# A graph network's diffusion layer: fp16 parts for the logits, keys by four tiles, and another order on TensorE, ScalarE and GpSimd

## What is computed

```python
q = X @ W1.T @ W2.T
k = X @ W3.T
logits = q @ k.T / TAU
probs = jax.nn.softmax(logits, axis=-1)
...
keep_sorted = cs - sp < TOP_P
...
for n in range(STEPS):
    A = _top_p_attention(Xa, W1, W2, W3)
    Xf = R @ Xf
    Xa = A @ Xa
    Z = Z + Xf @ U1[n].T + Xa @ U2[n].T
```

## Time and profile before

| | us |
|---|---|
| median of 3 runs | 3413.45 (3412.4 to 3425.25) |
| the profiled execution | 3413.29 |
| its span | 3411.6 |
| PE, PEld busy | 2529.9 (74%), 1807.8 (53%) |
| DVE, ACT, POOL busy | 2115.1 (62%), 1274.7 (37%), 618.0 (18%) |
| keys0, from 854.8 | 89.1 |
| step0, from 944.9 | 696.1 |
| keys1, from 1642.5 | 95.4 |
| step1, from 1738.9 | 928.1 |

### The profile page before, as it was taken

How to read it: one execution, slowest core, us unless ns; L and a number is a source line. 1 busy time by engine, 2 the same in 40 slices (tenths; PEclk the granted TensorE clock), 3 DMA queues, 4 the chain that set the end, 5 groups by cost and what they waited for, 6 DMA issues and landing times. The chain is left out here.

```text
span 3411.6 us, 47607 instructions
## 1 busy us (share of the span) xinstructions
PE 2529.9 (74%) x14938; PEld 1807.8 (53%) x14938; DVE 2115.1 (62%) x5159; ACT 1274.7 (37%) x2109; POOL 618.0 (18%) x1525
## 2 busy tenths in 40 slices
PE   3488888496848998887843596397757149999999
PEld 2366666385616776666622475275546124444458
DVE  5567777613236666675137777877776667777751
...
DMA packets 44330, 104.10 MB, mean 31 GB/s; under 512 B 5584, under 2 KB 24304, under 8 KB 41328
## 3 DMA queue, kind: packets, MB, share of 16 engines
...
## 5 line engine op out<-in xcount | busy, mean ns | idle before, releaser
L1206 PE MATMUL bank<-kT,step_queries 64*128 64x512 f32 x528 | 285.4, 693 | 315.0 <-ACT step_E L1273 299.5
L1705 DVE SCALAR_TENSOR_TENSOR fil_acc<-bank,fil_node,fil_acc 128x256 f32<-128x256 f32 x682 | 330.0, 484 | 108.6 <-PE bank L1778 96.0
L1206 PEld LDWEIGHTS bank<-kT,step_queries 64*128 64x128 f32 x528 | 107.5, 228 | 491.0 <-ACT step_E L1273 413.0
L1273 ACT ACTIVATE step_E<-bank 128x512 f32<-128x512 f32 (+1 forms) x264 | 137.5, 545 | 413.0 <-PE bank L1206 210.3
L1776 PE MATMUL bank<-fil_wh,fil_xTh 128*128 128x512 f16 x704 | 267.5, 380 | 0.0
L1777 PE MATMUL bank<-fil_wl,fil_xTh 128*128 128x512 f16 x704 | 267.3, 380 | 0.0
L1778 PE MATMUL bank<-fil_wh,fil_xTl 128*128 128x512 f16 x704 | 267.2, 380 | 0.0
L1293 ACT ACTIVATE step_junk<-step_E,step_first 128x2708 fp8e4<-128x2708 f32 x88 | 224.6, 2552 | 14.7 <-ACT step_bell L1300 8.9
L1386 DVE MAX8 step_top<-step_E 128x8 f32<-128x2708 f32 x44 | 131.2, 2982 | 133.1 <-ACT step_E L1273 128.6
L1223 PE MATMUL bank<-H,step_PT 128*128 128x256 f32 x968 | 212.6, 379 | 0.8 <-ACT step_PT L1264 0.8
L1223 PE MATMUL bank<-A,step_PT 128*128 128x256 f32 x968 | 212.6, 379 | 0.7 <-ACT step_PT L1264 0.7
...
## 6 DMA issues: line engine op xcount, KB each, us to landing
...
```

Source lines behind the costliest of these rows:

```text
L1206: pe.matmul(l_bank[n % 2][:, 0:m], queries[q][half, :], kT[half, c:c + m], start=True, stop=True).then_inc(l_ready, 1)
L1273: act.activation(E[q][j][:, c:c + m], l_bank[n % 2][:, 0:m], ACT.Copy).then_inc(l_done, 1)
L1705: c(dve.scalar_tensor_tensor(out=acc[k][:], in0=ps, scalar=node[k][:, n:n + 1], in1=acc[k][:], op0=ALU.mult, op1=ALU.add))
```

## The change

There are four parts.

1. `keys` stages four tiles at a time and, instead of kT and qT, keeps keys and queries as fp16 parts scaled by 64: kH and kL for the keys (high and low, the same 64 rows twice), and qHL, whose rows 0 to 63 are the high part of the query and rows 64 to 127 the low part. The second loop works on three tiles at a time, and the additions into H stand in the first loop.
2. `logits`: two fp16 products over 128 rows (qHL with kH, qHL with kL) for each fp32 one over 64; ACT scales by 1/4096 as it evacuates. POOL's `query` goes.
3. PE's order: two chunks of logits, a third of the neighbours, two chunks, a third, two chunks, a third, transposes, turn, half of attend, mix, the other half.
4. ACT's second sums stand ahead of the exponentials, and POOL's secant ahead of guess. The first sums are written at the head of the list with another lag.

DVE's list in `diffusion_step` is untouched. The diff, cut:

```diff
+            def product(n):
+                k, (b, m) = n % 2, CHUNKS[n]
+                w = m * 128
+                pe.wait_ge(xT_ready, n * 2 + 2)
+                pe.wait_ge(q1_done, n)
+                for c in range(2):
+                    last = pe.matmul(q1_bank[0:DA, 0:w], w1[:, c * DA:c * DA + DA], xT[k][:, c * BANK:c * BANK + w],
+                                     start=c == 0, stop=c == 1)
+                last.then_inc(q1_ready, 1)
...
+                pe.wait_ge(k_lo, n)
+                for c in range(2):
+                    last = pe.matmul(k_bank[:, 0:w], wk[:, c * 128:c * 128 + 128], xT[k][:, c * BANK:c * BANK + w],
+                                     start=c == 0, stop=c == 1)
+                last.then_inc(k_ready, 1)
+
+            def query(n):
+                k, (b, m) = n % 2, CHUNKS[n]
+                pe.wait_ge(q1_done, n + 1)
+                pe.wait_ge(q_lo, n)
+                pe.wait_ge(q_done, n)
+                pe.matmul(q_bank[:, 0:m * 128], w2[:], q1[k][:, 0:m * 128], start=True, stop=True).then_inc(q_ready, 1)
...
+            for n in range(NCH + 1):
+                if n < NCH:
+                    transposes(n)
+                if n > 0:
+                    query(n - 1)
+                    gram_sum(n - 1)
+                if n < NCH:
+                    product(n)
...
+            def high(n):
+                b, m = CHUNKS[n]
+                act.wait_ge(k_ready, n + 1)
+                act.activation(span(kH, b, m), k_bank[:, 0:m * 128], ACT.Copy, scale=SQ).then_inc(k_hi, 1)
+
+            def query_high(n):
+                b, m = CHUNKS[n]
+                act.wait_ge(q_ready, n + 1)
+                act.activation(span(qHL, b, m), q_bank[:, 0:m * 128], ACT.Copy, scale=SQ).then_inc(q_hi, 1)
...
+            def keep_query(n):
+                b, m = CHUNKS[n]
+                w = m * 128
+                dve.wait_ge(q_hi, n + 1)
+                part = qHL[DA:, b * 128:b * 128 + w]
+                dve.scalar_tensor_tensor(out=part, in0=q_bank[DA:, 0:w], scalar=SQ, in1=part,
+                                         op0=ALU.mult, op1=ALU.subtract).then_inc(q_lo, 1)
+                dve.tensor_scalar(qT[:, b * 128:b * 128 + w], q_bank[0:DA, 0:w], 1.0, None,
+                                  ALU.mult).then_inc(q_done, 1)
+
...
-            def query(p, q):
-                if not (isinstance(p, int) and p < 2):
-                    pool.wait_ge(l_ready, (p * 2 - 2) * NL)
-                pool.tensor_copy(queries[q][:], cols(qT, p, 128)).then_inc(q_ready, 1)
...
+            guess_0, guess_1 = ((0, lambda p, q, j=j: guess(p, q, j)) for j in range(2))
             if evals == 1:
-                pipelined(pool, [(-1, query), (0, lambda p, q: guess(p, q, 0)), (0, lambda p, q: newton(p, q, 0, final, aim, ready)),
-                                 (0, lambda p, q: guess(p, q, 1)), (0, lambda p, q: newton(p, q, 1, final, aim, ready))],
-                          T // 2)
+                newton_0 = (0, lambda p, q: newton(p, q, 0, final, aim, ready))
+                newton_1 = (1, lambda p, q: newton(p, q, 1, final, aim, ready))
+                pipelined(pool, [newton_1, guess_0, newton_0, guess_1], T // 2)
             else:
-                pipelined(pool, [(-1, query), (0, lambda p, q: guess(p, q, 0)), (1, lambda p, q: secant(p, q, 1, final, aim, ready)),
-                                 (0, lambda p, q: newton(p, q, 0, second, 0.0, aimed)),
-                                 (0, lambda p, q: guess(p, q, 1)), (0, lambda p, q: secant(p, q, 0, final, aim, ready)),
-                                 (0, lambda p, q: newton(p, q, 1, second, 0.0, aimed))], T // 2)
+                newton_0 = (0, lambda p, q: newton(p, q, 0, second, 0.0, aimed))
+                newton_1 = (1, lambda p, q: newton(p, q, 1, second, 0.0, aimed))
+                secant_0 = (0, lambda p, q: secant(p, q, 0, final, aim, ready))
+                secant_1 = (1, lambda p, q: secant(p, q, 1, final, aim, ready))
+                pipelined(pool, [newton_1, secant_1, guess_0, newton_0, secant_0, guess_1], T // 2)
...
-                half = slice(j * DA, j * DA + DA)
-                if n == 0 and j == 0:
-                    pe.wait_ge(q_ready, p + 1)
-                pe.matmul(l_bank[n % 2][:, 0:m], queries[q][half, :], kT[half, c:c + m],
-                          start=True, stop=True).then_inc(l_ready, 1)
-
-            def neighbours(p, j):
+                for part, k in enumerate((kH, kL)):
+                    last = pe.matmul(l_bank[n % 2][:, 0:m], cols(qHL, t, 128), k[:, c:c + m],
+                                     start=part == 0, stop=part == 1)
+                last.then_inc(l_ready, 1)
+
+            def neighbours(p, j, n):
                 t = p * 2 + j
-                moved(pe, a8_loaded, t, j)
-                reuse(pe, u_added, t)
-                core.fence(pe)
                 ps = pvf_bank[j][:, D:]
-                for part, ap in enumerate((hi, lo)):
-                    pe.matmul(ps, core.idh[:], ap(srcF, t), start=part == 0, stop=False)
-                adjacency_times(pe, ps, a8[j], srcF, start=False)
-
-            def attend(p, j):
+                if n == 0:
+                    moved(pe, a8_loaded, t, j)
+                    reuse(pe, u_added, t)
+                    core.fence(pe)
+                    for part, ap in enumerate((hi, lo)):
+                        pe.matmul(ps, core.idh[:], ap(srcF, t), start=part == 0, stop=False)
+                for i in range(T * n // 3, T * (n + 1) // 3):
+                    for part, ap in enumerate((hi, lo)):
+                        pe.matmul(ps, a8[j][:, i * 128:i * 128 + 128], ap(srcF, i), start=False,
+                                  stop=i == T - 1 and part == 1)
+
+            def attend(p, j, n):
                 t = p * 2 + j
-                pe.wait_ge(pT_done, t * NCH + NCH)
-                for i in range(T):
+                pe.wait_ge(pT_done, t * NCH + (NCH // 2 if n == 0 else NCH))
+                for i in range(T * n // 2, T * (n + 1) // 2):
                     last = pe.matmul(pvf_bank[j][:, 0:D], PT[:, i * 128:i * 128 + 128], srcA[:, i * D:i * D + D],
                                      start=i == 0, stop=i == T - 1)
-                last.then_inc(pv_ready, 1)
+                if n == 1:
+                    last.then_inc(pv_ready, 1)
...
-            def chunks(j):
-                for n in range(NL):
-                    yield 0, lambda p, q, n=n: logits(p, q, j, n)
+            def all_transposes(p, j):
                 for n in range(NCH):
-                    yield 2, lambda p, q, n=n: transposes(p, j, n)
-
-            pipelined(pe, [(2, lambda p, q: neighbours(p, 0)), *chunks(0), (3, lambda p, q: turn(p, 1)),
-                           (3, lambda p, q: mix(p, 1)), (2, lambda p, q: attend(p, 0)),
-                           (2, lambda p, q: neighbours(p, 1)), *chunks(1), (2, lambda p, q: turn(p, 0)),
-                           (2, lambda p, q: mix(p, 0)), (2, lambda p, q: attend(p, 1))], T // 2)
+                    transposes(p, j, n)
+
+            def half(j, mixed):
+                rows = [(2, lambda p, q, n=n: neighbours(p, j, n)) for n in range(3)]
+                chunks = [(0, lambda p, q, n=n: logits(p, q, j, n)) for n in range(NL)]
+                return [*chunks[0:2], rows[0], *chunks[2:4], rows[1], *chunks[4:], rows[2],
+                        (2, lambda p, q: all_transposes(p, j)), (mixed, lambda p, q: turn(p, 1 - j)),
+                        (2, lambda p, q: attend(p, j, 0)), (mixed, lambda p, q: mix(p, 1 - j)),
+                        (2, lambda p, q: attend(p, j, 1))]
+
+            pipelined(pe, [*half(0, 3), *half(1, 2)], T // 2)
...
-                act.activation(E[q][j][:, c:c + m], l_bank[n % 2][:, 0:m], ACT.Copy).then_inc(l_done, 1)
+                act.activation(E[q][j][:, c:c + m], l_bank[n % 2][:, 0:m], ACT.Copy,
+                               scale=1 / (SQ * SQ)).then_inc(l_done, 1)
...
+            products_0, products_1 = (2, lambda p, q: products(p, 0)), (3, lambda p, q: products(p, 1))
+            turned_0, turned_1 = ((2, lambda p, q, j=j: rows_turned(p, j)) for j in range(2))
+            logits_0, logits_1 = ((0, lambda p, q, j=j: all_evacuated(p, q, j)) for j in range(2))
+            exponentials_0, exponentials_1 = ((0, lambda p, q, j=j: exponentials(p, q, j)) for j in range(2))
+            first_0, first_1 = (0, lambda p, q: first_sums(p, q, 0)), (1, lambda p, q: first_sums(p, q, 1))
+            second_0, second_1 = (0, lambda p, q: second_sums(p, q, 0)), (1, lambda p, q: second_sums(p, q, 1))
             if evals == 1:
-                pipelined(act, [*chunks(0), (3, lambda p, q: products(p, 1)),
-                                (0, lambda p, q: exponentials(p, q, 0)), (0, lambda p, q: first_sums(p, q, 0)),
-                                *chunks(1), (2, lambda p, q: products(p, 0)),
```

(12 more changed lines are left out.)

258 lines of the change are left out of this document (138 added, 120 removed).

## The result

The changed kernel takes 3422.03 us (median of 20 runs, 3416.54 to 3424.92), the kernel before beside it 3413.47 (20 runs, 3409.8 to 3425.25). It lies inside the stated range of 3380 to 3545. The profiled execution has a span of 3422.9 against 3411.6.

The account below looks back on a forecast made before the run. PE was taken to bound step0, and a loop through DVE, ACT and POOL step1. 3413.3 - 36 (keys) - 57 (step0) + 147 (step1) = 3467 us; stated range 3380 to 3545, the forecast's own 3430 to 3505.

Parts of the forecast that it names:

- The nine repairs stay: Tie repairs: fp16 logits change little which rows lie near the boundary, so all nine remain; nothing in the sum.
- keys: Both key stages: four-tile groups, batches of three and additions under PE save 15 + 21 = 36 us, bounds 15 and 50.
- step0: First step: fp16 logits and PE's order cut the pitch from 26.09 to 22.4 us; -57, bounds -15 and -64.
- +147 of step1: Second step's whole term: +117 for 17 steady tiles, +10 for the others, +20 for PE's clock; bounds +78 and +200.
- some 16 of 22 tiles; the others run on other limits: In step0, only some 16 tiles gain 3.7 us each; those at both ends gain nothing.
- Rival D: fp16 parts move repairs: one more or less of nine, 20 us each, +-20 to 40; chance 0.05.
- The order of ACT and POOL: In step1, secant and guess are exposed: ACT's loop 31.4 us, 33.8 with holds, against 26.94; +117 over 17 tiles.
- Clock: In step1, PE at 1.2 GHz lengthens ACT's logits by up to 4.9 us in one tile in four: +20.
- A: Rival: in step1 the exponentials leave the chain, 23.9 us a tile, -52, total 3268; chance 0.10.
- B: Rival: step1's order costs less, loop 31.5 us without holds and at full clock, +78, total 3398; chance 0.17.
- C: Rival: PE's clock falls for good in step1, +200, total 3520 or more; chance 0.17.
- +200 end: Step1's upper bound, every tile 38.7 us, expected if the skill's clock rule holds for every tile.

Follow-up runs that it names:

- logits_twice: The changed kernel with each chunk of logits multiplied twice (four fp16 products, the second two overwriting the first two): 3494.72 us, ratio 1.0233.
- pe_old: The changed kernel with PE's order of the kernel before in both steps, fp16 logits kept: 3358.49 us, ratio 0.9841.
- largest_first: The changed kernel with ACT's and POOL's order of before in step1, and DVE's maximum ahead of its pass low there: 3273.0 us, ratio 0.9587.

## Why the prediction was right and wrong

**What failed is "The nine repairs stay", and the size of the gains in keys and step0.** The sum had -36 and -57 for keys and step0; measured are -47 and -82. The +147 of step1 came out at +138. Of the 45 us by which the total lies below the forecast, the two repairs that went are about 31 (14 in step0, 17 in step1), keys 11 and the rest of step0 11, while the rest of step1 came out 8 above its term. The 31 and what is worked out with it are estimates from intervals: with the two repairs the changed kernel would take some 3453, inside my own range of 3430 to 3505. Together these misses turn a forecast of 1.6% slower into no difference.

*step0.* The pitch was right: forecast 22.4, measured 22.6, and the reasoning (PE 3.7 less, ACT next) is borne out by logits_twice and pe_old. The step that failed is the count "some 16 of 22 tiles; the others run on other limits". The first five intervals, which ran at 22.5 to 24.4 before, gained 11 us as well; ten steady ones gained 34, the last five 13; the tile with the tie 18, of which 14 is the repair that no longer comes; the ends 7. (16 tiles by 3.7 are 59, not the 57 that I wrote.)

*The repairs.* "The nine repairs stay" is wrong: seven are left, and the sum had nothing for it. My reason was that the parts would change little which rows lie near the boundary; in fact two ties were gone in every run with the new arithmetic. Rival D named this, at 0.05 and some 20 us each, with its sign left open. What in the change moved them stays open.

*keys.* The first loop of keys0 went from 66.6 us to 51.5, the 15 I worked out, but the 5 that I gave back for longer groups didn't come, and the second loop fell by 7, not 5; 3 came back ahead of and behind the loops. In keys1 the further gain was partly the additions (2.8 by their run).

*The order of ACT and POOL.* The mechanism came as written, place by place: mass waits, guess behind secant, 31.4 us of list, holds and clock on top. I took 33.8; the twelve steady tiles without a repair have 35.5 to 39.7, 10.5 more than before, where I had 6.9 for each of 17 and the clock for one in four. Two prices were low. Holds: 2.4 on the mean, where in POOL's timeline 20 tiles have one of 2.6 to 3.0 on guess's first two instructions and eight a second one between the mass and the first sums. Clock: one tile in four by 4.9, where it is nearly every tile by 1.4 to 2.9. Against that, a repair adds 17 us to its tile (54.5 against 37.5) where it added 22 to 24 before, so the repaired tiles rose by 4 each and not by 6.9, and one repair is gone. So the term was near by errors of both signs, which is luck. Its bounds, +78 and +200, also left out the +10 of the first tiles that the term itself has.

*What I did not see.* I charged the whole of step1 to that order. Step1, nm to nm, in six kernels:

| ACT, POOL | PE | us |
|---|---|---|
| fp32 logits, before | before | 751.5 |
| fp32, new | before | 917.1 |
| fp16, before | before | 719.1 |
| fp16, new | before | 818.7 |
| fp16, before | new | 753.1 |
| fp16, new | new | 891.5 |

(The fp16 rows have the new keys too.) With every order of before, the change from fp32 to fp16 logits gives -32, of which 17 is the repair that went. With ACT's and POOL's new order it gives -98: there ACT's list is the bound, and from the first copy of logits to the end of the last it takes 6.9 us with fp32 and 4.2 with fp16. So the price of that order hangs on what else lies in ACT's list: 166 with fp32 logits, 100 with fp16, 138 with PE's new order too. PE's order costs 34 with ACT's and POOL's old one, and both together 172, 38 more than the sum of the two: thirds of neighbours then lie in ACT's list, and PE does the first of them at the lower clock, which is my reading of the 38 and not shown apart. In step0, where PE was the bound, the same order of PE is a gain of 14.

The rivals: A had the right wish in the wrong place; largest_first showed that even with ACT's list at 23.5 the pair's check holds. B is refuted: holds and clock both come. C's sign came in part: the third and fourth chunks of a tile are the first that PE multiplies after its wait, and they ran at 1.2 GHz in all 18 tiles read, the last two chunks in only four. But the clock didn't stay low (0.75 over step1), and it cost 1.4 to 2.9 us a tile and not 4.9. The Trainium skill (SBUF — State Buffer, "SBUF: two separate sides") says that a DVE instruction with two inputs from SBUF and one of GpSimd that reads SBUF lock each other out for the instruction's time; the 2.80 us beside keep's 3.04 agree. It also says (TensorE: Matmul & The Clock Gate, "HAM oscillation — how this bites in real kernels") that a loop whose compute is shorter than its wait starts cold on every pass. Here PE works longer in a tile than the 12 to 15 us that it waits, and still the trace shows the cold start in all 18 stretches of logits read. But step1 did not come out at the +200 end that I tied to it: mostly only the start of each pass was at 1.2 GHz, and keeping the clock up in 11 of them gave 23 us.
